# A decoder block on one core: slots 10 to 32 of the first phase in an order of their own on every engine

## What is computed

```
q = l2norm(silu(conv4(x @ Wq.T))) / DH ** 0.5        # one per token
k = l2norm(silu(conv4(x @ Wk.T)))                    # two per token
v = silu(conv4(x @ Wv.T))                            # two per token
beta = 2 * sigmoid(x @ Wb.T); g = -exp(A_log) * softplus(x @ Wa.T + dt_bias)
for t in range(T):                                   # per sequence and head
    state = state * exp(g_t)
    v_new = (v_t - k_t @ state) * b_t
    state = state + outer(k_t, v_new)
    o_t = q_t @ state
o = o * rsqrt(mean(o * o) + EPS) * o_norm_w * silu(x @ Wg.T)
x = layernorm(x + o @ Wo.T)
x = layernorm(x + cross_attention(x, ctx))           # second part
x = layernorm(x + ffn(x))                            # third part
```

## Time and profile before

| what | value |
|---|---|
| median of 3 runs | 1147.1 us (1144.97 to 1147.66) |
| profiled execution, its span (the page gives no other time of it) | 1150.4 us |
| PE busy | 1101.5 us, 96% |
| DVE busy | 818.0 us, 71% |
| ACT busy | 707.8 us, 62% |
| POOL busy | 472.0 us, 41% |
| mean granted TensorE clock | 0.985 |

### The profile page before, as it was taken

One profiled execution on the slowest core, in us unless ns is written; L12 is line 12 of the kernel. 1 busy time (PEld: TensorE's weight loads), 2 busy tenths in 40 slices (PEclk: granted clock), 3 DMA queues, 4 the chain that ended last, 5 costly groups with the idle time before them and its releaser, 6 DMA issues.

```text
span 1150.4 us, 28703 instructions
## 1 busy us (share of the span) xinstructions
PE 1101.5 (96%) x11420; PEld 763.6 (66%) x11420; DVE 818.0 (71%) x1429; ACT 707.8 (62%) x1243; POOL 472.0 (41%) x688
## 2 busy tenths in 40 slices
PE   8989799999999999999998899899999999999998
PEld 3444455555555555655554566679998999989987
DVE  5989769879779779779776756665666665655562
ACT  5777577687786777778676666554444444444433
POOL 1649484683882873964856512310000000110000
PEclk9999899999999999999998899999999999999999
DMA  4223345656565665666646332432222211112100
GB/s 131 56 63 88 86 73 86 132 106 101 126 94 110 124 115 96 133 138 143 141 88 219 103 121 66 134 95 51 51 53 67 51 48 47 47 48 50 29 19 10
DMA packets 164213, 101.82 MB, mean 89 GB/s; under 512 B 94289, under 2 KB 144593, under 8 KB 163185
## 3 DMA queue, kind: packets, MB, share of 16 engines
q1 hardware_dynamic: 162928, 99.78, 39.2%
q10 hardware_dynamic: 1152, 0.21, 0.1%
HBM read 62.72 MB, written 14.67 MB: 67 GB/s over the span
## 4 chain that ended last, share of the span: by engine, by line
PE 60%; DVE 12%; POOL 10%; issue 8%; ACT 4%; SPq 3%; DMA 3%; ACTq 0%; POOLq 0%; DVEq 0%
PE proj L581 13%; PE out L1792 5%; DVE conv L1213 5%; PE turned_v_chain L1792 5%; PE proj L1854 4%; PE turned_v_chain L1866 4%; PE proj L1731 4%; POOL inverse L1490 3%; POOL rank_one L1487 3%; PE gram L596 3%; PE gram L1766 2%; PE proj L1780 1%; PE turned_v_chain L587 1%; PE proj L1841 1%; PE out L605 1%
## 5 line engine op out<-in xcount | busy, mean ns | idle before, releaser
L1213 DVE SCALAR_TENSOR_TENSOR conv<-proj,kq_weights,conv 128x504 f32<-128x504 f32 (+2 forms) x261 | 189.7, 729 | 66.3 <-ACT conv L920 60.6
L581 PE MATMUL proj<-xT,vg_weights 128*128 128x512 f32 x384 | 194.1, 629 | 3.5 <-DMA vg_weights<-in_vg_w 2.2
L2109 POOL TENSOR_TENSOR rope<-rope_part,rope_part 128x512 f32<-128x512 f32 x32 | 42.1, 1336 | 321.5 <-DVE rope_part L2040 321.5
L581 PE MATMUL proj<-xT,kq_weights 128*128 128x512 f32 x348 | 167.7, 607 | 1.3 <-DVE conv L1213 1.0
L1213 DVE SCALAR_TENSOR_TENSOR conv<-proj,vg_weights,conv 128x504 f32<-128x504 f32 (+2 forms) x192 | 139.6, 728 | 26.4 <-ACT conv L920 23.3
L1490 POOL TENSOR_TENSOR inverse<-inverse,rank_one 128x30 f32<-128x30 f32 (+14 forms) x240 | 134.5, 560 | 18.8
L1487 POOL TENSOR_TENSOR rank_one<-inverse 128x30 f32<-128x30 f32 (+14 forms) x240 | 118.1, 492 | 22.9 <-DVE inverse L1274 8.0
L581 PEld LDWEIGHTS proj<-xT,kq_weights 128*128 128x128 f32 x348 | 62.4, 190 | 76.5 <-issue 64.0
L581 PEld LDWEIGHTS proj<-xT,vg_weights 128*128 128x128 f32 x384 | 66.9, 193 | 57.9 <-issue 50.0
L596 PEld LDWEIGHTS gram<-keys_q 128*64 128x64 f32 x896 | 56.8, 136 | 42.5 <-issue 24.9
L920 ACT ACTIVATE conv<-proj,kq_weights 128x512 f32<-128x512 f32 x87 | 59.6, 685 | 40.7 <-PE proj L581 40.3
(11 more groups left out here) (274 smaller groups left out, 2390.3 us busy)
## 6 DMA issues: line engine op xcount, KB each, us to landing
kq_weights<-in_kq_w SPq DMA_DIRECT2D x32, 390.0 KB, 6.5
vg_weights<-in_vg_w SPq DMA_DIRECT2D x32, 390.0 KB, 6.8
o_scratch<-oT SPq DMA_DIRECT2D x32, 256.0 KB, 2.2
o_in<-o_scratch SPq DMA_DIRECT2D x16, 512.0 KB, 4.1
o_rs<-o_rs_quarters SPq DMA_DIRECT2D x88, 64.0 KB, 6.1
diagonal<-gram_decayed SPq DMA_DIRECT2D x128, 32.0 KB, 2.0
inverse<-inverse SPq DMA_DIRECT2D x32, 128.0 KB, 2.8
q_first<-rope SPq DMA_DIRECT2D x128, 32.0 KB, 1.9
```

What stands on the lines that cost most here:

```text
L581: mm = e.matmul(bank(c, u)[:], w[:, (k * 3 + c % 3) * 128:(k * 3 + c % 3 + 1) * 128], xT[g][:, k, :], start=(k == 0), stop=(k == KD - 1))
L1213: e.scalar_tensor_tensor(acc(c, u)[:, :, back:], src[:, :, 0:S - back], weights(c, u)[:, j:j + 1], acc(c, u)[:, :, back:], ALU.mult, ALU.a ...
L2109: e.tensor_tensor(turned[half][:].rearrange("p b r q -> p r b q"), parts[2 * half][:], parts[2 * half + 1][:], op).then_inc(s_turned, 1)
```

## The change

In slots 10 to 32 (`woven(s)`), each of the five engine programs calls a function `woven_slot(s)` of its own in place of the common slot code. Nothing that is computed changes. What moves:

- PE: V0, both V turns, V1, prepare and G stand together; then norm, inverse low, the first gram half, high and low; then K0, K1 and Q together; then sum, output, the second gram half, and Y of the next unit (`chain_y(uc + 1)`), which stood at the head of the next slot.
- Banks: Q goes to the bank "decays", the V turns to the two gram banks, Y to the second half of VB.
- ACT, DVE, POOL and SP get orders that go with it, `CUTS` has four pieces in a slot, and the second half of the decays (`decay_gram(1, ...)`) moves to the next slot, between the steps of Q.

The core of the diff (the functions of the shared pieces, which only got names, are left out):

```diff
+CUTS = (((1, 1), (1, 1), (1, 1), (1, 5)), ((5, 10), (10, 13), (13, 14), (14, 16)),
+        ((16, 20), (20, 23), (23, 25), (25, 27)), ((27, 31), (31, 31), (31, 31), (31, 31)))
...
+        bank = lambda c, u: (OB if u < LAG else EB) if c == Q else P[0] if c in (V0, K0, G) else P[1]
+        woven = lambda s: LAG < s <= U
+        v_bank = lambda r, u: gram_bank[r] if woven(u + LAG + 1) else CH if (r, u) == (1, U - 1) else VB
+        y_bank = lambda u: VB[:, 256:512] if 1 <= u <= U - LAG else CH[:, 0:256]
...
+                def woven_slot(s):                       # PE
+                    project(V0, uc)
+                    e.wait_ge(s_silu[V1], ud + 1)
+                    e.wait_ge(s_gm, 4 * ub)
+                    turn_v(0, ud)
+                    turn_v(1, ud)
+                    e.wait_ge(s_conv[K1], 3 * (ub + 1))
+                    project(V1, uc)
+                        prepare(s, *prepare_at(s))
+                    e.wait_ge(s_conv[V0], 3 * (uc + 1))
+                    project(G, uc)
+                        norm(uo)
+                    chain_inverse_low(uc)
+                    gram(0, ub)
+                    chain_high_and_low(uc, ud)
+                        project(K0, ua)
+                        e.wait_ge(s_conv[V1], 3 * (uc + 1))
+                        project(K1, ua)
+                        e.wait_ge(s_whiout, uc + 1)
+                        project(Q, ua)
+                    chain_sum_low(uc)
+                    output(ud)
+                    e.wait_ge(s_gm, 4 * ub + 2)
+                    gram(1, ub)
+                        chain_y(uc + 1)
...
+                def woven_slot(s):                       # ACT
+                    copy_y(uc)
+                    silu(Q, ub, KQ[ub % 2][:, :, 0:S])
+                    tap(V0, uc)
+                    copy_v(0, ud)
+                    copy_v(1, ud)
+                    tap(V1, uc)
+                    silu(V0, uc, vT[uc % 2][:, :, :, 0])
+                        prepare_copy(*prepare_at(s))
+                    silu_gate(uc)
+                    copy_inverse_low(uc)
+                    silu(V1, uc, vT[uc % 2][:, :, :, 1])
+                        e.preload_act_table_set(LN_EXP)
+                    copy_w_high(uc)
+                    copy_w_low(ud)
...
+                        k_norms(h)
+                        tap(K0, ua)
+                    square_q(ub)
+                        tap(K1, ua)
+                        silu(K0, ua, keys(0, ua))
+                        tap(Q, ua)
...
+                def woven_slot(s):                       # DVE
+                    conv_step(Q, ub, 1)
+                        decay_gram(1, ub - 1)
+                    conv_step(Q, ub, 2)
+                        decay_queries(1, ub - 1)
+                    conv_step(Q, ub, 3)
+                    conv_step(V0, uc, 1)
+                        gate_output(uo)
+                    conv_step(V0, uc, 2)
+                    conv_step(V0, uc, 3)
+                    scan_decay(ub)
+                    conv_step(V1, uc, 1)
+                    conv_step(V1, uc, 2)
+                        prepare_rope(*prepare_at(s))
+                    conv_step(V1, uc, 3)
+                        solve_load(loading, 0)
+                    decay_gram(0, ub)
+                    decay_queries(0, ub)
+                        solve_load(loading, 1)
+                        solve_norms(loading)
+                        solve_turn(turning)
+                        solve_turn_again(turning)
+                        turn_k_norm(norming)
+                        convolve(K0, ua)
+                        conv_step(K1, ua, 1)
+                        conv_step(K1, ua, 2)
+                    less_sum(uc)
+                        conv_step(K1, ua, 3)
...
+                def woven_slot(s):                       # POOL
+                    eliminate(h, CUTS[cut][0])
+                    if cut == 3:
+                        scale_columns(h)
+                    decay_low(ub)
+                    eliminate(h, CUTS[cut][1])
+                    scale_w(ud)
+                        scale_rows(h)
+                    eliminate(h, CUTS[cut][2])
+                        scale_output(uo)
+                    eliminate(h, CUTS[cut][3])
+                    add_q_squares(ud)
```

More of the change, by code:

```diff
@@ L316, in delta_phase @@
         by_rows = lambda u: u < U - LAG - 1
-        v_bank = lambda r, u: CH if (r, u) == (1, U - 1) else VB
+        woven = lambda s: LAG < s <= U
+        gram_bank = [flat(GR[:, 2 * r:2 * r + 2, :]) for r in range(2)]
+        v_bank = lambda r, u: gram_bank[r] if woven(u + LAG + 1) else CH if (r, u) == (1, U - 1) else VB
+        y_bank = lambda u: VB[:, 256:512] if 1 <= u <= U - LAG else CH[:, 0:256]
+        high_bank = lambda u: high_chain if joined(u) and u > 0 else chain
         in_v_bank = lambda u: by_rows(u) or u + LAG + 2 > last_slot
@@ L471, in sync, with spread_root, store_output @@
                     e.dma_start(xT[g][:], a["xT"][:, :, g * GT:(g + 1) * GT]).then_inc(d_x[g], 16)
+                def spread_root(u):
+                    e.wait_ge(s_rs, u + 1)
+                    wait(e, s_gr, u)
+                    for j in range(4):
+                        e.dma_start(o_rs[:, j * TILE:(j + 1) * TILE],
+                                    rs4[RB * j:RB * j + 1, None, :].broadcast_to([1, 128, TILE])).then_inc(d_rs, 16)
+                def store_output(u):
+                    e.wait_ge(s_gr, u + 1)
+                    e.dma_start(o_scratch[:, 4 * group(u):4 * group(u) + 4, head(u), :],
+                                oT[u % 2][:].rearrange("v (t n) -> v t n", n=TILE)).then_inc(d_out[u % 2], 16)
@@ L472, in sync @@
                 for s in range(SLOTS):
+                    if woven(s):
+                        woven_slot(s)
+                        continue
                     ua, ub, uc, uo = s, s - 1, s - LAG, s - LAG - 2
-                    if live(uo) and by_rows(uo):
-                        e.wait_ge(s_rs, uo + 1)
-                        wait(e, s_gr, uo)
-                        for j in range(4):
-                            e.dma_start(o_rs[:, j * TILE:(j + 1) * TILE],
-                                        rs4[RB * j:RB * j + 1, None, :].broadcast_to([1, 128, TILE])).then_inc(d_rs, 16)
@@ L709, in chain_high @@
                     e.wait_ge(s_d10out, 2 * (u + 1))
-                    out = high_chain if joined(u) else chain
-                    if u == 0:
-                        e.wait_ge(s_ee, LAG)
+                    out = high_bank(u)
                     for b in range(GB):
@@ L1346, in vector @@
                         beta_turned()
-                    woven = LAG < s <= U
-                    if live(uc) and s > LAG and not (Y_BY_ACT and woven):
+                    if live(uc) and s > LAG:
                         copy_y(uc)
-                    loading, turning = (solve_at(s, n) if s > LAG else None for n in (5, 8))
+                    loading, turning = (solve_at(s, n) if s > U else None for n in (5, 8))
                     h = solve_at(s, 7)
@@ L1452, in vector @@
                         solve_turn_again(turning)
-                    if turning is not None and live(ud) and s > U:
-                        add_q_squares(ud)
+                        if live(ud):
+                            add_q_squares(ud)
                     if s == LAG:
@@ new lines, in scale_output, with add_rotated @@
+                def scale_output(u):
+                    e.wait_ge(s_og, u + 1)
+                    if by_rows(u):
+                        e.wait_ge(d_rs, 64 * (u + 1))
+                    else:
+                        e.wait_ge(s_rs, u + 1)
+                    e.tensor_tensor(oT[u % 2][:], oT[u % 2][:], o_rs[:], ALU.mult).then_inc(s_gr, 1)
+                def add_rotated(s):
+                    if prepare_at(s) is not None and prepare_at(s)[1] == KRS:
+                        e.wait_ge(s_pout, prepare_at(s)[0] + 1)
+                        e.tensor_tensor(t1[:], t1[:], t2[:], ALU.add).then_inc(s_padd, 1)
```

276 lines of the change are left out of this document (156 added, 120 removed).

## The result

The changed kernel takes 1236.65 us (median of 4 runs, 1232.29 to 1239.93) against 1147.38 us before (1144.97 to 1148.06): ratio 1.078, 95% interval 1.074 to 1.081, or 89 us more. The forecast was 1158, slower. The sign is right; the size is off by a factor of eight.

A forecast was written before the change was run, and what follows sets the result against it. A 20.04 us cycle over PE, ACT and DVE bounds the changed slots. With extras, slots 10 to 31 add 8.6 us and slot 32 1.9: 1150.4 + 10.5 = 1160.9, less 3.3 to the median: 1157.6, range 1140 to 1172.

The forecast's parts named there:

- the one costed at nothing: o_rs broadcasts at the end of SP's slot: land 6.1 us after issue, about 14 to 15 after G, no cost.
- cover of 1.5 us: POOL's scale_output, up to two eliminations and add_q_squares fit before the next norm on PE at 21.9, by some 1.5 us.
- POOL and SP fall behind as well: Rival: o_rs late, decay_low late in every slot, half a microsecond more each, 1170 us; inside the worse case, chance 0.20.
- the V0 cycle: Loop over PE, ACT and DVE from G through K0, Q and V0 to the next G; no slot shorter than 20.04 us.
- The cycle of 20.04: G to next G through K0, Q and V0 on PE, ACT and DVE: 20.04 us in a slot with nothing extra.
- its eight times: From G: K0's tap 7.34, steps 8.06, table load 10.36, Q's tap 12.24, step 12.96, V0's tap 16.49, step 17.21, G 20.04.
- Regular slot 20.0 to 20.3, turning 22: Expected sign in the profile after: a regular slot takes 20.0 to 20.3 us, one turning an inverse near 22.
- 0.4 us in a slot: PE, waiting at G for DVE's V0 steps, would idle 0.4 us in a slot.
- The term of 1.9 us for a turning slot: Slots 12, 16, 20, 24, 28: DVE's two inverse transposes end at 9.9, making K0's steps 1.9 us late; ends 0.8 and 2.9.
- Extras of loading and k norms: Slots loading diagonals cost 0.6 us more (ends 0 and 1.9), slots with k norms 0.55 more (ends 0 and 0.73).
- Ends: Slot 32, same order and a turning, adds 1.9 us to the +8.6 of slots 10 to 31.
- PE stays bound: Rival: PE sets the slot with 0.67 us less work, cycle shorter than 19.7; 1132, in part up to 1143 us; chance 0.18.

The follow-up runs named there:

- swap: The changed kernel with add_q_squares ahead of scale_output again on POOL; 1195.3 us, 1.041 of the kernel before.
- late: The changed kernel with scale_output a slot later on POOL, behind the next slot's decay_low, and its output store on SP with it; 1169.9 us, 1.020 of the kernel before.
- late_tap: Like late, and on ACT the tap of V0 ahead of silu of Q; 1149.5 us, 1.002 of the kernel before.

## Why the forecast was right in sign and wrong in size

- **The step that failed** is the one costed at nothing: "they land 6.1 us after issue, about 14 to 15 after G [...] That covers them by some 1.5 us." In the slot shown they landed 21.2 us after G (206.05 to 227.21). The 6.1 is the time of one DMA from its own issue. Four are issued one behind another by one queue, 6.23 us here and 3.9 to 4.1 in the slots on either side, and that comes on top; SP also had two stores of the inverse ahead. Exp ended near where it was expected, 8.0 after G against 7.3. So the cover of 1.5 us was a deficit of some 5 in this slot, and the sentence behind it, "without that cover each microsecond costs one", then did the rest. The sentence also names one way only, through add_q_squares. The other is the next slot's decay_low behind scale_output: swap cuts the first and gets 41 us back, late cuts both and gets 67. And "up to two eliminations" is four (3.0 to 4.0 us) in slots 13, 17, 21, 25 and 29.
- **What the trace of before had.** There the 22 groups of four took 4.1 us to issue (median, 3.7 to 4.8) and 10.3 from the first issue to the last landing (9.8 to 11.2). With exp at 7.3 they land at 17.6 and not at 14 to 15. By the prediction's own terms that is a deficit of some 1.6 us a slot, 35 us over 22 slots, and a forecast near 1193: an estimate, which leaves the stores of the inverse and decay_low out. One group, SP's queue before; its last DMA landed at 511.90:

```profile
501.53 4.23 SPq L478 DMA_DIRECT2D o_rs<-o_rs_quarters  x4
```

- **The rival "POOL and SP fall behind as well"** named the place (o_rs late, decay_low late), at 1170 for half a microsecond a slot and as a part of a 0.20 case. The mechanism was right; it was sized by a guess of 0.5 where the trace of before would have given 1.6 for the broadcasts alone. The diff and the text ahead of the prediction had the three facts needed: add_q_squares now behind scale_output, the broadcasts at the end of SP's slot, norm in PE's queue in front of high and low of the chain. They were not laid out as a loop of their own, as the V0 cycle was.
- **The cycle of 20.04** holds to 0.05 us in the slot shown for late and to 0.11 in the others with nothing extra (but for the two at 21.7), and each of its eight times to 0.11 in that slot. "Projections in run 1.72", "DVE idle 1.3 ahead of V0's first step, released by ACT's tap" (1.41), "table load waiting for K0 steps" (54.3 us in the changed kernel): all are there. "Regular slot 20.0 to 20.3, turning 22" fails for the changed kernel, where the other loop is longer, and holds for late. The "0.4 us in a slot" of idle PE does not: it is 1.1 in slot 11 of late, since that slot has less work for PE than the mean (before it took 19.57 us, and the forecast used 20.37 for all).
- **The term of 1.9 us for a turning slot** is about right as a size (21.5 to 21.9 from G to G), in part by luck. In slot 16 of late the transposes end and K0's steps start 9.5 after G, against the 9.9 forecast and 7.95 in the slot shown. But POOL's decay_low, which the prediction had starting at 4.5, starts at 1.4. What comes late is DVE's decay of the queries, at 5.4: it waits 0.47 for PE's high and low of the chain. The conclusion that I drew from it in the experiment, that the transposes should stand behind K0's steps, was wrong by sign.
- **Extras of loading and k norms**, 0.6 and 0.55: measured up to 1.0, and 0.4 to 0.6.
- **Ends**: slot 32 was priced at 1.9. In late, slots 32 to 35 cost 6.2 more than before (66.59 against 60.39 us from Y(23) to Y(27)) and slot 10 1.2 more. These two and the 3.1 over the 20 slots of the table, less the 1.9 priced, are 8.6. The sum was made in spans, where it came to 1160.9, and the span of late is 1169.4: 8.5 more. The other 3 us between 1158 and the median of late, 1169.9, are the difference of before's profiled execution to its median, which late does not have.
- **PE stays bound** (the case of the tiling rule) needed the cycle to be shorter than 19.7. With the tap moved it comes close: in late_tap PE is busy for 98% of the stretch and idles 0.3 us in a slot.
- **TensorE's clock** was not in the forecast. From Y(1) to Y(24) the same 5432 matmuls keep PE busy for 475.0 us in the changed kernel and for 457.1 in late: its own work is 18 us longer at a granted clock of 0.95 instead of 0.98. PE also idles for 73 of the 548 us there (26 of 483 in late), so how much of the 18 reaches the time isn't shown.

## What to carry to other kernels

When an order is rewritten, draw the loop of every value that leaves an engine and comes back in the next slot, the small ones through DMA too, and add its steps as one adds those of the main cycle; "hidden" is a claim about a sum, not about a step. Several DMAs that one instruction waits for cost the sum of their issues plus one flight (4.1 and 6.3 us in the median of the kernel before, not 6.1 in all), on a queue that has other work in front. An instruction that waits for such a landing belongs behind everything on its engine that someone else needs soon: moving one of 1.3 us a slot later, with the store that waits for it, was worth 67 us here. And only the longest loop pays: an edit worth 20 us in one version was worth nothing in the other.

## What the hardware showed that was not expected

PE's wait of 3.28 us at the norm is followed by work at half the clock. Two stretches of the changed kernel, the wait and what follows it, and two of late around a G that took 3.38 us instead of 1.86 (length, busy us, then granted clock):

```profile
228.67:233.80 5.13, 1.88 (x5) 0.57 (x4) 2.98 (x4) 1.40 (x3) 4.58 (x10) 0.91 0.74 163
233.83:237.70 3.87, 3.87 (x56) 2.99 (x56) 0.00 (x0) 2.11 (x4) 3.32 (x8) 0.50 0.79 227
```

```profile
321.00:325.20 4.20, 2.66 (x14) 1.24 (x12) 2.82 (x5) 2.92 (x5) 3.73 (x7) 1.00 0.64 128
325.20:328.50 3.30, 3.30 (x4) 0.97 (x4) 3.23 (x4) 0.93 (x2) 2.14 (x4) 0.56 0.38 141
```

In the first pair PE was busy for 1.88 of 5.13 us and then had a clock of 0.50, the lower of its two levels, 1.2 GHz: norm takes 0.58 instead of 0.36 and half a gram 2.33 instead of 1.24. In the second it had been busy for 2.66 of 4.20 us, and the slot of late costs 1.6 more than its equals. The same is seen at 410.13, where G takes 3.00 us; these are the two slots at 21.7 in the table. In both, PE had waited twice, for 0.66 and 0.88 us, right ahead of G. The Trainium skill, "TensorE: Matmul & The Clock Gate", section "The HAM clock gate", says that the clock has these two levels and that the idle state is the slow one. The trace agrees, at 0.50. So the wait of 3.28 us on PE cost some 5: 0.22 more for norm, 0.37 for inverse low and 1.09 for the half gram came behind it.

Four DMAs of 64 KB each took between 3.9 and 7.4 us to issue on SP in the changed kernel, 4.1 in the median. In many groups the first three take 0.5 to 0.6 us each and the fourth 2.1 to 2.2; single issues took up to 3.4. The last of a group landed 4.4 to 6.3 us after its issue had ended. The Trainium skill, "DMA: Bandwidth & Descriptors", section "Rules for kernel authors", says that spreading DMAs over the issuing engines brings no bandwidth and saves only the sequencer's issue time. Issue time is 4 us and more of each turn of this loop, but no run here issued any of the four elsewhere, so what that would save is not shown.
